# Hyperbolic attention loop: ScalarE takes roots, logarithms and exponentials of two steps at a time, and the value products stand one chunk every second unit

## What is computed

```python
def _L1_attn_ref(x, Wq, Wk, Wv, Wo):
    q, k, v = split_heads(x @ Wq.T), split_heads(x @ Wk.T), split_heads(x @ Wv.T)
    diff_sq = jnp.maximum(q_norm_sq + k_norm_sq - 2.0 * qk, 0.0)
    denom = jnp.maximum((1.0 - q_norm_sq) * (1.0 - k_norm_sq), 1e-06)
    cosh_arg = jnp.maximum(1.0 + 2.0 * diff_sq / denom, 1.0)
    distance = jnp.where(cosh_arg > 1.0, jnp.arccosh(...), 0.0)
    attn = jax.nn.softmax(-distance, axis=-1)
    out = jnp.einsum('bhnm,bhmd->bhnd', attn, v)
    return merge_heads(out) @ Wo.T
```

## Time and profile before

| | |
|---|---|
| median of 3 runs | 1372.44 us (1369.58 to 1375.97) |
| profiled execution, its own time | 1376.86 us |
| its span | 1374.8 us |
| busy share of the span, PE / DVE / ACT / POOL | 72% / 68% / 55% / 38% |
| the hyperbolic loop in the span | from 715 to 1209 us |

### The profile page before, as it was taken

The page is one execution under the profiler, slowest core; times in us unless marked ns, Lnnn a source line. Parts: engine busy times, 40 slices in busy tenths (PEclk is TensorE's granted clock), DMA queues, the critical chain, the costliest instruction groups (busy, mean ns, idle before and its releaser), DMA issues. The chain is left out here.

```text
span 1374.8 us, 17643 instructions
## 1 busy us (share of the span) xinstructions
PE 989.0 (72%) x5593; PEld 503.7 (37%) x5593; DVE 941.6 (68%) x2073; ACT 762.5 (55%) x986; POOL 526.4 (38%) x418
## 2 busy tenths in 40 slices
PE   5886822589999737999275678898778887346276
PEld 2552221256666436999120011111111111035266
DVE  5676598368888273445578988999999997255401
ACT  4204513226666512444153599999999999921021
POOL 0000000200000005664154887888788878100263
PEclk9998955659999857999575555555665555565597
DMA  4001000113110005664224100000010000021245
GB/s 144 0 0 28 0 0 19 67 37 98 43 36 25 9 31 175 210 210 152 76 87 139 46 23 34 35 24 23 32 38 23 23 23 0 0 64 36 56 131 140
DMA packets 59291, 80.26 MB, mean 58 GB/s; under 512 B 13185, under 2 KB 36541, under 8 KB 58945
## 3 DMA queue, kind: packets, MB, share of 16 engines
q1 hardware_dynamic: 50208, 67.33, 15.7%
q0 software_dynamic: 3968, 8.13, 2.0%
q10 hardware_dynamic: 5024, 3.67, 0.8%
HBM read 63.56 MB, written 15.34 MB: 57 GB/s over the span
## 5 line engine op out<-in xcount | busy, mean ns | idle before, releaser
L2485 POOL TENSOR_TENSOR hb_t<-hb_t,hb_r 128x512 f32<-128x512 f32 x248 | 364.3, 1507 | 70.8 <-ACT hb_r L2301 70.8
L2498 DVE TENSOR_SCALAR hb_dpos<-hb_psR 128x1024 f32<-128x1024 f32 x128 | 155.7, 1217 | 27.0 <-PE hb_psR L2229 18.5
L2250 PE MATMUL hb_psO<-hb_t,ha_va 128*9 128x512 f32 x512 | 114.8, 997 | 61.2 <-ACT hb_t L2324 61.2
L2238 PE MATMUL hb_psR<-ha_q,ha_k 20*128 20x512 bf16 x256 | 126.5, 593 | 43.2 <-DVE hb_dpos L2498 43.2
L2506 DVE SCALAR_TENSOR_TENSOR hb_t<-hb_psR,hb_dpos 128x1024 f32<-128x1024 f32 x128 | 155.1, 1212 | 0.0
L1843 ACT ACTIVATE ga_att<-ga_psB 128x512 f32<-128x512 f32 (+3 forms) x256 | 102.2, 453 | 78.2 <-PE ga_psB L1775 73.7
L1864 DVE TENSOR_REDUCE ga_nm<-ga_psA 128x1 f32<-128x128 f32 (+3 forms) x256 | 114.4, 485 | 35.8 <-PE ga_psA L1751 32.3
L2229 PE MATMUL hb_psR<-ha_q,ha_k 78*128 78x512 bf16 x256 | 127.4, 600 | 9.1 <-DMA ha_k<-hsx 4.6
L2324 ACT ACTIVATE hb_t<-hb_t 128x4096 f32<-128x4096 f32 x32 | 113.8, 3603 | 0.0
L2515 DVE SCALAR_TENSOR_TENSOR hb_r<-hb_t 128x1024 f32<-128x1024 f32 x64 | 104.9, 1638 | 0.0
L1625 POOL MEMSET ga_q<- 64x8192 bf16 x1 | 6.9, 6920 | 251.2 <-POOLq L1552 251.2
(11 more groups left out here) (469 smaller groups left out, 2233.4 us busy)
## 6 DMA issues: line engine op xcount, KB each, us to landing
m2x_e_w<-in_L_ffn_W_dram SPq DMA_DIRECT2D x78, 256.0 KB
m1x_e_w<-in_L_ffn_W_dram SPq DMA_DIRECT2D x23, 256.0 KB
ga_q<-qx SPq DMA_DIRECT2D x48, 96.0 KB
ha_q<-hqx SPq DMA_DIRECT2D x48, 96.0 KB
ha_k<-hkx SPq DMA_DIRECT2D x16, 288.0 KB
hy_fwd<-in_const_fwd_dram SPq DMA_DIRECT2D x1, 2048.0 KB
f_down<-in_L_ffn_W_dram ACTq DMA_DIRECT2D x4, 512.0 KB, 4.2
hsx<-hp_aparts SPq DMA_DIRECT2D x6, 288.0 KB, 4.6
```

What stands on the lines that cost most here:

```text
L2238: mm = pe.matmul(psR[:, side_slot(n), i, :], k[SIDE:SIDE + SROWS, it % 2, i0 + i, P * c:P * c + P], q[SIDE:SIDE + SROWS, it % 2, i0 + i, : ...
L2250: mm = pe.matmul(psO[32 * i:32 * i + VW, :], va[:, CH * (it // G) + c, HPG * (it % G) + i, :], t[:, (2 * it + c % 2) % T_QUADS, 2 * (c // ...
L2485: half_sum = pool.tensor_tensor(tt, tt, rr, ALU.add)
L2498: dve.tensor_scalar(dpos[:, n % 2, :], psR[:, dist_slot(n), :, :].rearrange("p i t -> p (i t)"), 0.0, None, ALU.max).then_inc(dpos_ready, 1)
```

## The change

ScalarE's loop goes over pairs of steps: roots of both, one table load, logarithms and exponentials of both, one table load. `copy_batch` moves behind the pair. The value products move from units 23, 24, 27 and 28 to units 24, 26, 28 and 30, and what follows them on TensorE and VectorE moves by one to three units.

```diff
-            VALUES_AT = (23, 24, 27, 28)
-            COPY_AT, TURN_AT, OUTPUT_AT = 28, 31, 31
-            A_TURN_AT, PROJECT_AT, ADD_AT = 34, 38, 38
-            DRAIN = 40
+            VALUES_AT = (24, 26, 28, 30)
+            COPY_AT, TURN_AT, OUTPUT_AT = 31, 33, 33
+            A_TURN_AT, PROJECT_AT, ADD_AT = 35, 39, 39
+            DRAIN = 41
...
-                    for it in range(STEPS + 3):
-                        if it < STEPS:
+                    for first in range(0, STEPS, 2):
+                        for it in (first, first + 1):
                             product_roots(it)
                             two_roots(it)
-                        if 1 <= it < STEPS + 1:
-                            act.preload_act_table_set("natural_log_exp_and_others")
-                            logs(it - 1, 0)
-                        if it >= 3 and (it - 3) % G == G - 1:
-                            copy_batch((it - 3) // G)
-                        if 1 <= it < STEPS + 1:
-                            logs(it - 1, 1)
-                            weights(it - 1, 0)
-                            weights(it - 1, 1)
+                        act.preload_act_table_set("natural_log_exp_and_others")
+                        logs(first, 0)
+                        logs(first, 1)
+                        weights(first, 0)
+                        weights(first, 1)
+                        logs(first + 1, 0)
+                        weights(first + 1, 0)
+                        logs(first + 1, 1)
+                        weights(first + 1, 1)
+                        if first >= G and first % G == 0:
+                            copy_batch(first // G - 1)
+                    copy_batch(BATCH - 1)
```

## The result

The changed kernel takes 1411.49 us (median of 4 runs: 1403.1, 1404.05, 1418.92, 1419.88), the kernel before 1373.1 us beside it: ratio 1.0286, 95% interval 1.0254 to 1.0318. It is slower, as forecast, but by 38 us where the forecast said 13, and outside its range of 1375 to 1397. The runs lie in two groups 15 to 16 us apart.

The account below looks back on a forecast made before the run. ScalarE set the pace before; after, a circle through GpSimd's 32 sums would bound each pair at 57.7 us. Start +14.7, six pairs +15.8, last pair -17.8 gave +12.7 on 1372.44: 1385.5 us, range 1375 to 1397.

Parts of the forecast that it names:

- the circle PR, 32 sums, L1, W1, load, PR: From a pair's first product root (PR) through GpSimd's sums, last logarithm (L1) and exponential (W1): 51.7 + 1.0 n us.
- 57.7: Forecast us per pair of steps, with six products beside GpSimd's sums; 55.16 before.
- n: Number of a pair's eight products that fall beside GpSimd's run of sums, each adding 1.0 us; forecast 6.
- the start: Loop's start up to PR(2), the first root of step 2: 14.7 us later than before.
- the last pair: From the root PR(14) to the last exponential: 52.1 us against 69.9 before, so -17.8 us.
- The value products cost nothing: Moving the value products on TensorE: claimed to cost nothing, TensorE's work staying 23.56 us a step.
- 4 us for the collisions of VectorE's four sums: In the last pair, VectorE's own four sums may hold up GpSimd by some 4 us.
- what a collision costs when sums run for 45 us at a stretch: Listed unknown, a VectorE product meeting GpSimd's sums: rows give 0.97 to 1.07 us, -1 to +3 us over six pairs.
- My placement: Placing a pair's eight products in time from the waits: six inside GpSimd's run of sums, the last two outside.
- T: Start of PR(f), the first product root of a pair's even step f, from which the placement counts us.
- the six pairs: From PR(2) to PR(14): 347.7 us, `copy_batch` included, against 331.9 before, so +15.8 us.
- VectorE or TensorE gets late: Rival: stalls at ring `r` and at the values eat VectorE's 5.8 us slack; pair up to 4 us longer, 1400 us; chance 0.05.

Follow-up runs that it names:

- e7: Changed kernel, GpSimd waiting for its own last sum ahead of every form of 8 sums: 1389.82 us, ratio 1.0117 to the kernel before.
- e8: Changed kernel with GpSimd pauses, VectorE adding two of the four units of form 1 of every odd step instead of GpSimd: 1374.34 us, ratio 1.0013.
- e3: Kernel before with ScalarE's old order, only the value products moved to units 24, 26, 28 and 30: 1371.84 us, ratio 0.9986.
- e1: Changed kernel, VectorE's wait for GpSimd's sums moved from before `product` to before `clipped` of the same turn: 1422.22 us, ratio 1.0361.
- e2: Changed kernel with ScalarE's new order kept, the value products back at units 23, 24, 27 and 28: 1401.27 us.
- e9: Kernel before, each step's first product from step 2 on waiting for 8 of the 16 sums then running: 1436.7 us.
- e11: Kernel before, each step's first product from step 2 on waiting for 12 of 16 sums, GpSimd pausing at each form's start: 1497.15 us.
- e6: Kernel before, each step's first product from step 2 on waiting for 6 of the 16 sums then running: 1403.1 us.

## Why the prediction was wrong in size

**Right.** 15 loads are gone, and the circle PR, 32 sums, L1, W1, load, PR replaces ScalarE's own work as the bound of a pair. In pairs that no long product touches it was sized well: the pair from 938.91, whose run of sums took 46.40 us, is 58.7 long, the one from 1129.11 59.5, and the one from 1071.42 57.7, a 2.5 us wait for a late product included, where I had 57.7. n, the products beside a run, is 6 or 7 by the lengths 45.38, 46.40 and 46.72 us ((length - 39.4) / 1.0). e7 bears the mechanism out by its waits and e8 by its cure. In the profiled execution of the changed kernel the start was +15.6 (PR(2) at 809.96 less the first root, 70.6, against 55.0; forecast +14.7), the last pair 51.3 us, -18.6 (from 1188.61 to the end of the last exponential at 1239.90; forecast -17.8). The value products cost nothing (e3). In the last pair I had 4 us for the collisions of VectorE's four sums; one of them was passed over instead, GpSimd's 24 sums took their bare 29.52 us, and ScalarE had no idle time.

**Wrong.** The step that failed is the one that I listed last among the unknowns: "what a collision costs when sums run for 45 us at a stretch. The rows give 0.97 to 1.07 us." Every collision in the rows of before happens within a run of 16 sums of which about four are met; there no product finds more than six sums back to back ahead of it. The changed order makes runs of 32, and in two of its six pairs eight and nine sums are done before a product comes. The one at 1014.14 starts 12.8 us behind the start of its run at 1001.31, the one at 827.11 starts 11.1 us after the last product before it (813.99 to 816.01). By the table one product in 14 is passed over behind eight sums and 12 in 14 behind ten, in e1 all three behind eight to ten, and in e2 one of three behind eight or nine. So what such a product costs is in part chance. In the same profile the product at 1146.62, with seven sums ahead of it and released by GpSimd as well, got in at once:

```profile
1146.62 2.21 DVE L2518 SCALAR_TENSOR_TENSOR hb_r<-hb_t 128x1024 f32<-128x1024 f32 x1 [1.01 <-POOL hb_t L2488]
```

In the clean pair the products of VectorE's timeline stand closer:

```profile
944.32 1.89 DVE L2518 SCALAR_TENSOR_TENSOR hb_r<-hb_t 128x1024 f32<-128x1024 f32 x1
948.39 1.27 DVE L2518 SCALAR_TENSOR_TENSOR hb_r<-hb_t 128x1024 f32<-128x1024 f32 x1
958.44 2.07 DVE L2518 SCALAR_TENSOR_TENSOR hb_r<-hb_t 128x1024 f32<-128x1024 f32 x1
```

From the end of the second to the third are 8.8 us, seven sums. So I priced the wait at 1.0 us, by the nearest rows, and it was up to 28 us: 21 more sums of 1.23 us, and the product. My placement already held the warning: a run from T+3.7 whose first product comes at T+16 to T+17 (the trace has T+17.2 and T+16.5) is a stretch of nine or ten.

The parts of the result. In the profiled execution the six pairs are 46.8 us longer than before: six clean ones of 58.7 would be 20.3 longer (forecast 15.8), and the two long products added 1.6 + 10.0 + 15.1 = 26.7, less 0.2 in the two last pairs. Start, pairs and last pair make 15.6 + 46.8 - 18.6 = 43.8 us; the spans differ by 42.0, since the loop's first root came 3.8 us earlier than in the profile before and what follows the last exponential took 2.1 us longer. In the medians the circle is 16 us by e7's ratio of 1.0117, its pauses of some 0.5 us a pair included (forecast 13), and the passed-over products are the 22 us between 1411.5 and 1389.8. That one or two of them an execution make the two groups of run times, and none, one, one and two e2's 1388, 1401, 1401 and 1420 us, is inferred: only the profiled executions were seen, with two such products in the changed kernel and one in e2's 1401.44.

The rival "VectorE or TensorE gets late", which I gave 0.05 and 1400 us, came true in its symptom, ScalarE waiting for VectorE at a root, though its cause was another: I reckoned VectorE's lateness from its busy time, and no rival had a price for one instruction that is locked out.

The Trainium skill ("SBUF — State Buffer", Who interferes with whom) has VectorE and GpSimd share a pair of SBUF ports as an exclusive lock, held for the whole instruction, with the other engine fully blocked meanwhile. The products of 2.1 to 2.2 us beside 1.23-us sums agree. That a blocked product gets in once the instruction that blocks it ends does not hold in these runs: one waited through 21 sums, and the measurement decides.

## What to carry to other kernels

Before grouping instructions of one engine to save table loads, trace the circle of waits that the grouping closes: a saving of 1.4 us a load can be lost when the last item of a batch of GpSimd work releases the first of the next batch. When the mean of a group is higher than its known kinds of instruction can make it, or a kernel's runs fall into groups, ask for the longest single instruction and look at what ran beside it. Where back-to-back GpSimd additions meet a VectorE instruction with its sources and target in SBUF, as here, break GpSimd's stretches up by a wait for its own last result (0.18 us): one ahead of every eight sums took 22 us off the changed kernel.

## What the runs showed of the hardware

A VectorE instruction with its sources and its target in SBUF (128x1024), meeting back-to-back GpSimd additions (128x512), waits at most for the one in progress (up to 2.3 us in all) after up to 6 unmet ones, and after 10 to 12 nearly always for all that are queued, up to 27.98 us; a GpSimd pause of 0.18 us resets the count. 8 and 9 lie between (1 of 14 in e9, 2 of 2 in the changed kernel, 1 of 3 in e2), and 10 still does (12 of 14). It holds for `product`, whose two sources are one tile, and for VectorE's own addition of two tiles (12.93 us behind 14 unmet sums in the changed kernel). Why GpSimd's additions go on ahead then, the runs do not say; I only know that VectorE's idle time before (e1, e11) and the kind of release (e6, e11; VectorE's own addition was released by ScalarE) are not it. Other lengths of sums were not tried. `clipped`, which reads PSUM, and `ratio`, which reads PSUM and one tile of SBUF, kept their 1.20 to 1.23 us everywhere, also beside sums.
